# Summing two halves of the squared features on TensorE instead of GpSimd, in the last stage of a fused sequence kernel

## The chip, the cores and the metric

The kernel runs on one core of one Trainium2 chip. The metric is the device time of one execution in microseconds (us); lower is better. The core has five engines that work side by side, each through its own instructions in order: TensorE (PE, with its weight loads listed as PEld), VectorE (DVE), ScalarE (ACT), GpSimd (POOL) and SyncE (SP), which issues DMAs. They wait for each other on semaphores.

## The reference, cut to what matters

Four blocks work on 16 sequences of 256 tokens with 128 channels. The last one, which takes two thirds of the time, is six layers of local attention with l2-normalised queries and keys, and a gated feed-forward layer:

```python
def l2norm(t):
    return t / jnp.maximum(jnp.linalg.norm(t, axis=-1, keepdims=True), 1e-12)

def attn_layer(x, Wqkv, qs, ksc, Wo):
    qkv = x @ Wqkv                      # 16 heads of 64 features for q, k, v
    q, k, v = jnp.split(qkv, 3, -1)
    ...
    q = l2norm(q) * qs
    k = l2norm(k) * ksc
    ...                                 # rotary, scaled by position
    out = local_attention(q, k, v)      # windows of 32, each looks one back
    return out @ Wo

for i in range(DEPTH):                  # DEPTH = 6
    x = attn_layer(shift_tokens(x), ...) + x
    x = ffn_layer(shift_tokens(x), ...) + x
```

The norm of each query and key needs the sum of the squares of its 64 features. That sum is what the change touches.

## The kernel before, in words

The last stage ("phase d") takes the 6 layers times 16 sequences as 96 items n. Every engine runs a loop over turns f, and in a turn works on several items at different steps: the projection of item f and of item f-1, the attention of f-2 and f-3, the feed-forward of f-3 and f-4. The order of the work within a turn is written out by hand, one list of calls for each engine. Nothing is scheduled at run time: an engine goes through its list and stands still at a call whose semaphore isn't there yet.

For one item the projections come in 8 chunks (`CHUNKS`), 4 for keys and 4 for queries. A chunk is a bank of PSUM, 128 rows by 512: 4 heads with 32 features each in the rows, and in the columns two halves of 256 tokens, features 0 to 31 and features 32 to 63 of the same heads. The sum of squares runs through these calls:

- `project` (PE, L1516): 6 matmuls into the chunk's bank.
- `squares` (ACT, L1286): squares the whole bank into one of four buffers `d_sq[i % 4]`, 128 by 2 halves by 256; signals `s_sq`. For the second four chunks it waits until the first four have been summed (`s_sm`).
- `add_halves` (POOL, L1449): adds the second half of the buffer onto the first, 128 by 256; signals `s_sa`.
- `sum_squares(n, m)` (PE, L1527): for the four chunks of `m`, four matmuls with a 128x32 stationary matrix of ones and zeros (`sel`), which add up the 32 rows of each head. Each writes its own 32 columns of the array (`tile_position=(0, g * WIN)`) and its own 32 rows of bank 7. Both values of `m` accumulate there. Signals `s_sm`.
- `norm_rsqrt` (ACT, L1294 to L1296), `norm_weight`, `norm_factor`, `norm_split` (DVE, L1069, L1075, L1082) and `spread_norms` (PE, L1538) turn the sums into factors for the keys, which `scale_keys` (DVE, L1097) applies.

POOL also adds the two products of the rotary step (`rotary_sums`, L1441), scales the scores (`scale_shifted`, L1458), and scales the probabilities (`softmax_scale`, L1464). `rotary_products` (DVE, L1061) waits for `rotary_sums` three chunks back. The rotated queries and keys go to their places by DMAs from SP (L1757 for keys, L1766 for queries), and `scores` (PE, L1549, L1556) waits for them.

In PE's list a turn begins with `turn_tokens` (L1503). `sum_squares(f - 1, 1)` stands before `attention(f - 3, 1)` (L1601), and `sum_squares(f, 0)` between `token_products(f - 2, 5)` and `token_products(f - 2, 6)` (both L1583). `token_products(., 6)` waits for `ffn_scale` of DVE (L1154) as well. Where a new layer begins, ACT and POOL have extra work in their lists: `weights_high`, `tables`, `head_matrices` and `split_low`.

Of the kernel before, what the change touches and what calls it, by code (L numbers as in the profile page):

```python
# [21 lines left out]
ALU = mybir.AluOpType  # L22
# [4 lines left out]
SEQS, T = 16, 256  # L27
# [8 lines left out]
WIN = 32  # L36
# [35 lines left out]
def build(nc, dram, out):  # L72
    ctx = ExitStack()
    with ctx:
        def sb(name, shape, dt=F32):
            return ctx.enter_context(nc.sbuf_tensor(name, shape, dt))
# [5 lines left out]
        bank = [psum[:, i, :] for i in range(8)]  # L82
# [11 lines left out]
        sel = sb("sel", [P, 2, WIN])  # L94
# [708 lines left out]
        def phase_c_tensor(pe):  # L803
# [85 lines left out]
            def sequence_turns(n, s, left):  # L889
# [39 lines left out]
        CHUNKS = 8  # L929
        KS = 3  # L930
        d_xt = [ld(T) for _ in range(3)]
        d_sq = [ld(2, T) for _ in range(4)]
# [19 lines left out]
        base_stage = tab_flat[:, 4 * TPS * DH:4 * TPS * DH + 4 * TPS * P].rearrange("p (k t r f) -> p k t r f", k=4, t=TPS, r=4)  # L952

        (s_sel, s_basep, s_base, s_zk, s_normed, s_zero, s_stats, kept,
         s_xtp, s_xt, s_split, s_proj, s_sq, s_sa, s_xh, s_rp, s_ad, s_sm, s_y, s_r, s_zh, s_z, s_rq, s_R, s_mR, s_dk, s_dq,
         s_s, s_sub, s_rm, s_exp, s_inv, s_prob, s_pt, s_u, s_uev, s_at, s_x2, s_x2p, s_xf, s_mean, s_xsq, s_var,
         d_chain, d_act_chain, s_y2, s_xc, s_xn, s_up, s_gl, s_h, s_ffo, s_x_done, s_m, s_mvo, s_whi, s_wlo, s_tab,
         loaded_qk, loaded_sc, loaded_vo, loaded_w1, loaded_w2) = (
            sem("d_" + s) for s in (
                "sel basep base zk normed zero stats kept "  # L960
                "xtp xt split proj sq sa xh rp ad sm y r zh z rq R mR dk dq "
                "s sub rm exp inv prob pt u uev at x2 x2p xf mean xsq var "
                "chain act_chain y2 xc xn up gl h ffo x_done m mvo whi wlo tab "
                "loaded_qk loaded_sc loaded_vo loaded_w1 loaded_w2").split())
# [6 lines left out]
        def at_least(eng, s, count):  # L971

            if count >= 1:
                eng.wait_ge(s, count)

        def here(n):

            return 0 <= n <= LAST

        def layer_of(n):  # L980
            return n // SEQS
# [40 lines left out]
        def split_low(pool, l, *chunks):  # L1022

            for i in chunks:
                pool.wait_ge(s_whi, CHUNKS * l + i + 1)
                hi, staged = split_high(i)
                lo = wqk_split[:, i, 1, :, :].rearrange("p h (r f) -> p h r f", r=4)
                nc.gpsimd.tensor_tensor(lo, staged, hi.bitcast(F32), ALU.subtract).then_inc(s_wlo, 1)
# [402 lines left out]
        def phase_d_gpsimd(pool):  # L1431
            def rotary_sums(n, *chunks):
                if not here(n):
                    return
                for i in chunks:
                    c = CHUNKS * n + i
                    pool.wait_ge(s_rp, c + 1)
                    if i % 4 == 0:
                        at_least(pool, (s_dk, s_dq)[i // 4], 128 * n)
                    t = d_t[c % KS]  # L1440
                    nc.gpsimd.tensor_tensor(d_rot[i // 4][:, i % 4, :, :], t[:, :, 0, :], t[:, :, 1, :], ALU.add).then_inc(s_ad, 1)  # L1441

            def add_halves(n, *chunks):
                if not here(n):
                    return
                for i in chunks:
                    pool.wait_ge(s_sq, CHUNKS * n + i + 1)
                    sq = d_sq[i % 4]
                    nc.gpsimd.tensor_tensor(sq[:, 0, :], sq[:, 0, :], sq[:, 1, :], ALU.add).then_inc(s_sa, 1)  # L1449

            def scale_shifted(n, h):
                if not here(n):
                    return
                pool.wait_ge(s_sub, 2 * n + h + 1)
                pool.wait_ge(s_rq, n + 1)
                e = d_e[h].rearrange("p (w r) k -> p w r k", w=WPT)
                factor = d_rq[:, WPT * h:WPT * h + WPT, :].rearrange("p w (r m) -> p w r m", m=8)[:, :, :, 4:5]
                nc.gpsimd.tensor_tensor(e, e, factor.to_broadcast([P, WPT, QUADS, 2 * WIN]), ALU.mult).then_inc(s_rm, 1)  # L1458

            def softmax_scale(n, h):  # L1460
                if not here(n):
                    return
                pool.wait_ge(s_inv, 2 * n + h + 1)
                nc.gpsimd.tensor_tensor(d_e[h], d_e[h], d_inv[h].unsqueeze(2).to_broadcast([P, 4 * QUADS, 2 * WIN]), ALU.mult)\  # L1464
                    .then_inc(s_prob, 1)

            nc.gpsimd.memset(d_k, 0.0).then_inc(s_zk, 1)  # L1467
            nc.gpsimd.memset(d_u[:, 0], 0.0).then_inc(s_zk, 1)
            for f in range(TURNS_D):
                fresh = here(f) and f and f % SEQS == 0  # L1470
                next_fresh = here(f + 1) and (f + 1) % SEQS == 0
                rotary_sums(f - 1, 0, 1)
                add_halves(f - 1, 4)
                rotary_sums(f - 1, 2, 3)
                add_halves(f - 1, 5)
                rotary_sums(f - 1, 4)
                add_halves(f - 1, 6, 7)
                rotary_sums(f - 1, 5)
                scale_shifted(f - 2, 0)
                rotary_sums(f - 1, 6, 7)  # L1480
                scale_shifted(f - 2, 1)
                if fresh:
                    split_low(pool, layer_of(f), 4, 5, 6, 7)
                add_halves(f, 0, 1, 2, 3)
                if next_fresh:
                    split_low(pool, layer_of(f + 1), 0, 1, 2, 3)
                softmax_scale(f - 2, 0)
                softmax_scale(f - 2, 1)

        def phase_d_tensor(pe):  # L1490
# [29 lines left out]
            def sum_squares(n, m):  # L1520
                if not here(n):
                    return
                pe.wait_ge(s_sa, CHUNKS * n + 4 * m + 4)
                if m == 0:
                    at_least(pe, s_mR, 2 * n)
                for g in range(4):
                    last = nc.tensor.matmul(bank[7][g * WIN:(g + 1) * WIN, 0:T], sel[:, m, :], d_sq[g][:, 0, :],  # L1527
                                            start=(m == 0), stop=(m == 1), skip_group_check=True,
                                            tile_position=(0, g * WIN))
                last.then_inc(s_sm, 1)  # L1530

            def spread_norms(n, h):
# [142 lines left out]
            for k in range(4):  # L1675
                for t in range(TPS):
                    last = nc.tensor.transpose(bank[k][:, t * P:(t + 1) * P], base_stage[:, k, t, :, :].rearrange("p r f -> p (r f)"),
                                               ident[:, :])
# [5 lines left out]
            for f in range(TURNS_D):  # L1684
# [8 lines left out]
                project(f - 1, 7)  # L1693
                scores(f - 2, 1)
                sum_squares(f - 1, 1)
                attention(f - 3, 1)
                if here(f - 2) and (f - 2) % SEQS == 0:
# [14 lines left out]
                project(f, 4)  # L1712
                token_products(f - 2, 5)
                sum_squares(f, 0)
                token_products(f - 2, 6)
                token_products(f - 2, 7)
# [161 lines left out]
        @block.gpsimd  # L1878
        def _(pool):
            with pool.Fori(0, SA) as step:  # L1880
                phase_a_gpsimd_steps(pool, step)
            end_phase(pool, 1)
            phase_d_constants(pool)
            split_first(pool)
            end_phase(pool, 2)
            end_phase(pool, 3)
            phase_d_gpsimd(pool)
            end_phase(pool, 4)
# [112 lines left out]
```

## Time and profile before

| | |
|---|---|
| median of 3 runs | 4386.15 us (4378.98 to 4389.12) |
| the profiled execution's own time | 4383.15 us |
| its span in the profile | 4381.4 us |
| PE busy | 3982.0 us, 91% |
| DVE busy | 3434.9 us, 78% |
| ACT busy | 2610.2 us, 60% |
| POOL busy | 2353.6 us, 54% |

These shares are over the whole span. The last stage begins at about 1457 us; before it POOL has hardly anything to do. So the stage has to be read by itself. A busy PE is one that has a matmul under way; the ends of matmuls are modelled, so the start of one group of matmuls to the start of the next is a better measure of what a group takes than the sum of its durations. A float32 matmul leaves two records in the trace: four matmuls of `sum_squares` are a row with x8.

### The profile page before, as it was taken

Reading aid. Unit: us, or ns where it says so; the run is one execution under the profiler, and the core shown is the slowest. Engines: PE = TensorE matmul, PEld = TensorE weight load, DVE = VectorE, ACT = ScalarE, POOL = GpSimd, SP = SyncE. Lnnn points to the kernel's source line nnn. Section 1 sums busy time; section 2 is a strip of 40 time slices with the busy share of each in tenths; the row PEclk is TensorE's granted clock in tenths of the full one; section 3 lists DMA queues with packets and bytes.
Section 4 is the critical chain, followed back from the end, with each engine's and each line's share of the span. In section 5 each row is a group of like instructions: output and inputs, shape, how many; then the busy total and the mean of one; then the engine's idle time right before and its main releaser. Section 6 shows DMA issues by size and latency. Waiting matters only on the chain.

```text
span 4381.4 us, 119305 instructions
## 1 busy us (share of the span) xinstructions
PE 3982.0 (91%) x47524; PEld 2662.6 (61%) x47524; DVE 3434.9 (78%) x5294; ACT 2610.2 (60%) x5495; POOL 2353.6 (54%) x2019
## 2 busy tenths in 40 slices
PE   3335998999999599999999999999999999999997
PEld 1112444666666467667676677767666767767765
DVE  6775112666666699998999899989999899989996
ACT  2332333666665466676666666676666666666665
POOL 0001000000000488887888788878888778878884
PEclk7667999999999799999999999999999999999999
DMA  3000000000000233332432332333332343332333
GB/s 100 0 0 0 0 0 0 1 1 0 0 0 1 58 92 69 79 76 65 101 76 64 79 95 67 78 71 91 79 79 64 77 101 69 70 79 68 72 79 78
DMA packets 264306, 238.63 MB, mean 54 GB/s; under 512 B 31494, under 2 KB 259979, under 8 KB 263051
## 3 DMA queue, kind: packets, MB, share of 16 engines
q1 hardware_dynamic: 263818, 231.76, 22.7%
q8 instruction: 352, 5.77, 0.6%
q14 instruction: 136, 1.11, 0.1%
HBM read 26.13 MB, written 4.19 MB: 7 GB/s over the span
## 4 chain that ended last, share of the span: by engine, by line
PE 71%; DVE 4%; ACT 4%; issue 2%; SPq 1%; POOL 1%; DMA 1%; DVEq 0%; ACTq 0%; POOLq 0%
PE bank L1583 15%; PE bank L1516 13%; PE bank L1601 8%; PE bank L1556 7%; PE bank L1643 6%; PE bank L1656 2%; PE bank L1549 2%; PE bank L854 2%; PE bank L819 2%; PE bank L843 2%; PE bank L1527 2%; ACT arena L753 2%; PE bank L832 2%; PE bank L824 2%; PE bank L863 1%
## 5 line engine op out<-in xcount | busy, mean ns | idle before, releaser
L1061 DVE TENSOR_TENSOR arena<-bank,tab 128x1024 f32<-128x1024 f32 x768 | 937.0, 1221 | 193.5 <-ACT arena L1286 135.8
L1441 POOL TENSOR_TENSOR arena<-arena 128x512 f32<-128x512 f32 x768 | 1009.9, 1331 | 42.0 <-DMA arena<-arena 40.6
L1583 PE MATMUL bank<-m_vo,arena 128*32 128x512 f32 x6144 | 756.9, 599 | 17.3 <-DVE arena L1154 11.0
L1286 ACT ACTIVATE arena<-bank 128x512 f32<-128x512 f32 x768 | 457.9, 596 | 526.5 <-PE bank L1516 517.7
L1516 PE MATMUL bank<-x_split,wqk_split 128*128 128x256 f32 x4608 | 720.3, 299 | 25.9 <-DVE arena L1061 11.9
L1516 PEld LDWEIGHTS bank<-x_split,wqk_split 128*128 128x128 f32 x4608 | 605.3, 192 | 175.0 <-issue 85.6
L1449 POOL TENSOR_TENSOR arena<-arena 128x256 f32<-128x256 f32 x768 | 556.3, 735 | 170.1 <-ACT arena L1286 169.8
L1310 ACT ACTIVATE arena<-bank 128x512 f32<-128x512 f32 x768 | 457.0, 596 | 186.4 <-PE bank L1583 183.7
L1467 POOL MEMSET arena<- 128x4608 f32 x1 | 3.9, 3947 | 1039.4 <-DVEq L150 1039.4
L1458 POOL TENSOR_TENSOR arena<-arena 128x1024 f32<-128x1024 f32 x192 | 372.1, 1938 | 262.7 <-DVE arena L1109 262.7
L1464 POOL TENSOR_TENSOR arena<-arena 128x1024 f32<-128x1024 f32 x192 | 373.3, 1945 | 127.3 <-DVE arena L1122 127.0
L1556 PE MATMUL bank<-arena 128*32 128x128 f32 x12288 | 403.7, 273 | 0.4 <-issue 0.4
L1601 PE MATMUL bank<-arena 128*32 128x128 f32 x12288 | 372.1, 273 | 0.0
L1556 PEld LDWEIGHTS bank<-arena 128*32 128x32 f32 x12288 | 345.8, 110 | 37.2 <-issue 0.8
L1601 PEld LDWEIGHTS bank<-arena 128*32 128x32 f32 x12288 | 331.9, 110 | 31.2 <-issue 0.7
L1583 PEld LDWEIGHTS bank<-m_vo,arena 128*32 128x32 f32 x6144 | 158.8, 109 | 260.7 <-ACT arena L1310 140.6
L753 ACT ACTIVATE arena<-bank,arena 128x256 f32<-128x256 f32 x512 | 235.8, 473 | 106.2 <-DVE arena L673 92.1
L1643 PE MATMUL bank<-arena,w 128*128 128x256 f32 (+1 forms) x1152 | 282.2, 381 | 0.9 <-ACT arena L1341 0.8
L398 PE MATMUL bank<-ident,arena 128*128 128x128 f32 x160 | 39.6, 414 | 238.3 <-DVE arena L294 136.7
L1129 DVE STREAM_TRANSPOSE arena<-arena 128x1024 f32<-128x1024 f32 x192 | 235.1, 1224 | 26.6 <-POOL arena L1464 26.6
L1103 DVE TENSOR_REDUCE arena<-bank 128x16 f32<-128x1024 f32 x192 | 234.3, 1220 | 14.3 <-PE bank L1556 6.4
L1097 DVE TENSOR_TENSOR arena<-arena,bank 128x1024 f32<-128x1024 f32 x192 | 232.8, 1212 | 2.7 <-PE bank L1538 2.7
(236 smaller groups left out, 6991.4 us busy)
## 6 DMA issues: line engine op xcount, KB each, us to landing
arena<-arena SPq DMA_DIRECT2D x1536, 128.0 KB, 2.5
wqk_stage<-in_wqk SPq DMA_DIRECT2D x6, 1024.0 KB, 8.3
out_x<-x_all SPq DMA_DIRECT2D x8, 512.0 KB, 4.9
wvt<-in_wvt SPq DMA_DIRECT2D x6, 512.0 KB, 4.3
wo<-in_wo SPq DMA_DIRECT2D x6, 512.0 KB, 5.4
arena<-in_wbh SPq DMA_DIRECT2D x1, 2048.0 KB, 9.4
arena<-out_x SPq DMA_DIRECT2D x4, 512.0 KB, 6.0
w<-in_w SPq DMA_DIRECT2D x6, 341.0 KB, 5.9
```

The source lines that it names most:

```text
L1061: nc.vector.tensor_tensor(d_t[c % KS].rearrange("p k h t -> p k (h t)"), bank[c % 2][:, :].unsqueeze(1).to_broadcast([P, 2, 2 * T]), tab[: ...
L1286: nc.scalar.activation(d_sq[i % 4].rearrange("p h t -> p (h t)"), bank[c % 2][:, :], ACT.Square).then_inc(s_sq, 1)
L1310: nc.scalar.activation(d_u[:, 1 + w, :, :], bank[U_BANK[w]][:, :].rearrange("p (a c) -> p a c", a=QUADS), ACT.Copy).then_inc(s_uev, 1)
L1441: nc.gpsimd.tensor_tensor(d_rot[i // 4][:, i % 4, :, :], t[:, :, 0, :], t[:, :, 1, :], ALU.add).then_inc(s_ad, 1)
L1449: nc.gpsimd.tensor_tensor(sq[:, 0, :], sq[:, 0, :], sq[:, 1, :], ALU.add).then_inc(s_sa, 1)
L1458: nc.gpsimd.tensor_tensor(e, e, factor.to_broadcast([P, WPT, QUADS, 2 * WIN]), ALU.mult).then_inc(s_rm, 1)
L1464: nc.gpsimd.tensor_tensor(d_e[h], d_e[h], d_inv[h].unsqueeze(2).to_broadcast([P, 4 * QUADS, 2 * WIN]), ALU.mult)\
L1516: last = nc.tensor.matmul(bank[c % 2][:, h * T:(h + 1) * T], wqk_split[:, i, wp, h, :], x_split[:, n % 2, xp, :], start=(q == 0), stop=(q ...
L1556: last = nc.tensor.matmul(bank[2 + b][g * WIN:(g + 1) * WIN, (2 * v + a) * P:(2 * v + a + 1) * P], d_q[:, a, g, at:at + WIN], d_k[:, a, g, ...
L1583: last = nc.tensor.matmul(bank[U_BANK[w]][g * WIN:(g + 1) * WIN, :], d_xt[n % 3][:, w * WIN:(w + 1) * WIN], m_vo[:, 4 * g:4 * g + 4, :].re ...
L1601: last = nc.tensor.matmul(bank[6][v * WIN:(v + 1) * WIN, h * C:(h + 1) * C], d_pt[h][:, at, :], d_u[:, WPT * h + v + z, r, :], start=(r == ...
L1643: last = nc.tensor.matmul(bank[UP_BANK[c]][0:m, half * T:(half + 1) * T], w1_of(n)[:, first + c * P:first + c * P + m], d_xn, start=True, ...
```

## The change

`add_halves` is taken out of POOL's list, with its semaphore `s_sa`. `sum_squares` waits for the squares themselves (`s_sq`) and issues eight matmuls in place of four: four over the first halves and four over the second, all in the same accumulation. Nothing else changes.

```diff
-            def add_halves(n, *chunks):
-                if not here(n):
-                    return
-                for i in chunks:
-                    pool.wait_ge(s_sq, CHUNKS * n + i + 1)
-                    sq = d_sq[i % 4]
-                    nc.gpsimd.tensor_tensor(sq[:, 0, :], sq[:, 0, :], sq[:, 1, :], ALU.add).then_inc(s_sa, 1)
...
                 rotary_sums(f - 1, 0, 1)
-                add_halves(f - 1, 4)
                 rotary_sums(f - 1, 2, 3)
-                add_halves(f - 1, 5)
                 rotary_sums(f - 1, 4)
-                add_halves(f - 1, 6, 7)
                 rotary_sums(f - 1, 5)
                 scale_shifted(f - 2, 0)
                 rotary_sums(f - 1, 6, 7)
                 scale_shifted(f - 2, 1)
                 if fresh:
                     split_low(pool, layer_of(f), 4, 5, 6, 7)
-                add_halves(f, 0, 1, 2, 3)
...
-                pe.wait_ge(s_sa, CHUNKS * n + 4 * m + 4)
+                pe.wait_ge(s_sq, CHUNKS * n + 4 * m + 4)
                 if m == 0:
                     at_least(pe, s_mR, 2 * n)
-                for g in range(4):
-                    last = nc.tensor.matmul(bank[7][g * WIN:(g + 1) * WIN, 0:T], sel[:, m, :], d_sq[g][:, 0, :],
-                                            start=(m == 0), stop=(m == 1), skip_group_check=True,
-                                            tile_position=(0, g * WIN))
+                for half in range(2):
+                    for g in range(4):
+                        last = nc.tensor.matmul(bank[7][g * WIN:(g + 1) * WIN, 0:T], sel[:, m, :], d_sq[g][:, half, :],
+                                                start=(m == 0 and half == 0), stop=(m == 1 and half == 1), skip_group_check=True,
+                                                tile_position=(0, g * WIN))
                 last.then_inc(s_sm, 1)
```

PE's list around the second `sum_squares` of a turn (L1527), before; x is the number of matmuls in a row, and `arena` holds all the buffers:

```order
L1656 MATMUL bank<-w,arena 128x128 x6
L1516 MATMUL bank<-x_split,wqk_split 128x256 x6
L1583 MATMUL bank<-m_vo,arena 32x512 x4
L1527 MATMUL bank<-arena,sel 32x256 x4
L1583 MATMUL bank<-m_vo,arena 32x512 x8
L1503 MATMUL bank<-ident,x_all 128x128 x2
```

and the same place of the changed kernel, where the line numbers are 11 or 12 lower (`sum_squares` is L1516 there and `token_products` L1572):

```order
L1645 MATMUL bank<-w,arena 128x128 x6
L1504 MATMUL bank<-x_split,wqk_split 128x256 x6
L1572 MATMUL bank<-m_vo,arena 32x512 x4
L1516 MATMUL bank<-arena,sel 32x256 x8
L1572 MATMUL bank<-m_vo,arena 32x512 x8
L1491 MATMUL bank<-ident,x_all 128x128 x2
```

The four matmuls have become eight at the same place, and no other row of PE has moved.

POOL's list over one turn, before (L1441 is `rotary_sums`, L1449 `add_halves`):

```order
L1464 TENSOR_TENSOR arena<-arena 128x1024 x2
L1441 TENSOR_TENSOR arena<-arena 128x512 x2
L1449 TENSOR_TENSOR arena<-arena 128x256
L1441 TENSOR_TENSOR arena<-arena 128x512 x2
L1449 TENSOR_TENSOR arena<-arena 128x256
L1441 TENSOR_TENSOR arena<-arena 128x512
L1449 TENSOR_TENSOR arena<-arena 128x256 x2
L1441 TENSOR_TENSOR arena<-arena 128x512
L1458 TENSOR_TENSOR arena<-arena 128x1024
L1441 TENSOR_TENSOR arena<-arena 128x512 x2
L1458 TENSOR_TENSOR arena<-arena 128x1024
L1449 TENSOR_TENSOR arena<-arena 128x256 x4
```

and of the changed kernel (L1450 is `scale_shifted` there, L1456 `softmax_scale`):

```order
L1456 TENSOR_TENSOR arena<-arena 128x1024 x2
L1441 TENSOR_TENSOR arena<-arena 128x512 x6
L1450 TENSOR_TENSOR arena<-arena 128x1024
L1441 TENSOR_TENSOR arena<-arena 128x512 x2
L1450 TENSOR_TENSOR arena<-arena 128x1024
```

Eight additions of a turn are gone, and the six first rotary sums stand next to each other.

## Rows read from the trace of the kernel before

**Rows 1.** Busy time by engine: first turns, steady turns, last turns.

```profile
core 0: us, PE busy (x) PEld busy (x) DVE busy (x) ACT busy (x) POOL busy (x), PEclk, DMA share, GB/s
1457.00:1560.00 103.00, 78.06 (x832) 54.61 (x832) 68.61 (x72) 56.31 (x100) 64.67 (x60) 0.80 0.27 61
1560.00:4293.00 2733.00, 2701.36 (x40280) 1902.49 (x40272) 2492.63 (x3037) 1860.80 (x3510) 2208.58 (x1881) 1.00 0.34 78
4293.00:4381.40 88.40, 64.13 (x948) 42.96 (x944) 48.95 (x65) 40.98 (x70) 29.43 (x21) 0.89 0.29 74
```

**Rows 2.** PE in order of time, one turn: start us, us, line.

```profile
2485.54 0.44 PE L1503 MATMUL bank<-ident,x_all 128*128 128x128 f32 x2
...
2512.49 0.61 PE L1527 MATMUL bank<-arena,sel 128*32 128x256 f32 x8
2512.92 1.90 PE L1583 MATMUL bank<-m_vo,arena 128*32 128x512 f32 x16
2514.75 0.44 PE L1503 MATMUL bank<-ident,x_all 128*128 128x128 f32 x2
...
2526.60 0.60 PE L1527 MATMUL bank<-arena,sel 128*32 128x256 f32 x8
2527.03 1.92 PE L1601 MATMUL bank<-arena 128*32 128x128 f32 x64
```

**Rows 3.** PE's longest waits from 1550 to 4250 us: total, times, longest.

```profile
PE bank L1583 <- DVE arena L1154: 9.9, 10, 1.1
PE bank L1623 <- ACT arena L1310: 4.5, 5, 0.9
```

**Rows 4.** Groups by line in the last stage: busy, mean ns, idle before.

```profile
L1449 POOL TENSOR_TENSOR arena<-arena 128x256 f32<-128x256 f32 x764 | 553.4, 735 | 143.9 <-ACT arena L1286 143.6
...
L1527 PE MATMUL bank<-arena,sel 128*32 128x256 f32 x1536 | 118.2, 382 | 1.5 <-POOL arena L1449 1.5
...
L1527 PEld LDWEIGHTS bank<-arena,sel 128*32 128x32 f32 x1536 | 47.0, 110 | 58.4 <-issue 55.0 <-POOL arena L1449 3.3
```

**Rows 5.** The chain that ended last, around 4240 us: start us, us.

```profile
4232.73 0.43 PE bank L1527 x8
...
4246.84 0.43 PE bank L1527 x8
```

**Rows 6.** Weight loads in order of time, at the second group of rows 2.

```profile
2526.49 0.23 PEld L1527 LDWEIGHTS bank<-arena,sel 128*32 128x32 f32 x8
```

**Rows 7.** PE in order of time, two turns where a layer begins.

```profile
1909.05 0.61 PE L1527 MATMUL bank<-arena,sel 128*32 128x256 f32 x8
1910.57 0.64 PE L1583 MATMUL bank<-m_vo,arena 128*32 128x512 f32 x4 [0.91 <-DVE arena L1154]
...
1940.58 0.61 PE L1527 MATMUL bank<-arena,sel 128*32 128x256 f32 x8
1942.26 1.92 PE L1583 MATMUL bank<-m_vo,arena 128*32 128x512 f32 x16 [1.06 <-DVE arena L1154]
```

**Rows 8.** From the sums to the spread norms, steady turn, in order of time.

```profile
2527.28 0.39 ACT L1294 ACTIVATE arena<-bank 128x256 f32<-128x256 f32 x1 [0.51 <-PE bank L1527]
...
2532.53 0.48 DVE L1082 SCALAR_TENSOR_TENSOR z_split<-z_split,odd,arena 128x256 fp32r<-128x256 f32 x1
...
2533.41 0.48 PE L1538 MATMUL bank<-z_split,sel_r 128*128 128x256 f32 x2
```

**Rows 9.** The chain that ended last, in the first turns of the stage.

```profile
1470.20 1.06 PE bank L1527 x8
...
1478.73 0.73 POOL arena L1449
1479.51 1.12 PE bank L1527 x8
...
1505.73 0.73 POOL arena L1449
```

**Rows 10.** The same chain, where the last item is projected.

```profile
4302.00 0.74 POOL arena L1449
...
4303.57 0.74 POOL arena L1449
```

More of the change, by code:

```diff
@@ L954, in build @@
         (s_sel, s_basep, s_base, s_zk, s_normed, s_zero, s_stats, kept,
-         s_xtp, s_xt, s_split, s_proj, s_sq, s_sa, s_xh, s_rp, s_ad, s_sm, s_y, s_r, s_zh, s_z, s_rq, s_R, s_mR, s_dk, s_dq,
+         s_xtp, s_xt, s_split, s_proj, s_sq, s_xh, s_rp, s_ad, s_sm, s_y, s_r, s_zh, s_z, s_rq, s_R, s_mR, s_dk, s_dq,
          s_s, s_sub, s_rm, s_exp, s_inv, s_prob, s_pt, s_u, s_uev, s_at, s_x2, s_x2p, s_xf, s_mean, s_xsq, s_var,
@@ L960, in build @@
                 "sel basep base zk normed zero stats kept "
-                "xtp xt split proj sq sa xh rp ad sm y r zh z rq R mR dk dq "
+                "xtp xt split proj sq xh rp ad sm y r zh z rq R mR dk dq "
                 "s sub rm exp inv prob pt u uev at x2 x2p xf mean xsq var "
```

## The prediction

> **What bounds the kernel now.** I read the busy times by stretch first [rows 1]. From 1560 to 4293 us PE is busy for 2701.36 of 2733 us, 99%, at a granted clock of 1.00, that is 2.4 GHz. DVE stands at 91%, POOL at 81%, ACT at 68%. In the stretches ahead of it and behind it PE is busy for three quarters of the time, at mean granted clocks of 0.80 and 0.89: these are waits for a chain through all engines. Only 31.64 us of the long stretch (2733.00 less 2701.36) have no matmul.
>
> Busy time alone isn't proof, since ends of matmuls are modelled. So I read PE in order of time [rows 2]. One turn takes 29.21 us (from 2485.54 to 2514.75), and its groups start one behind the other with no wait listed. The list of PE's waits agrees: between 1550 and 4250 us the longest two entries are 9.9 us and 4.5 us in total [rows 3], 10 and 5 times, at the beginnings of layers. And the chain that ended last goes through `sum_squares` itself, 0.43 us each time [rows 5]. The reader is to see a PE that sets the pace, with an addition on POOL that nobody on the path waits for: PE's matmuls of `sum_squares` waited for it for 1.5 us and their weight loads for 3.3 us, over the whole stage [rows 4].
>
> **The change part by part.**
>
> *Removed: 768 additions of POOL*, 735 ns each [rows 4], about 564 us of POOL's time and nearly 6 us of a turn. In the steady turns it is worth nothing, since POOL isn't what PE waits for. What it can give there is at most the few microseconds just named.
>
> *Removed: the wait on `s_sa`*, replaced by one on `s_sq`, which comes earlier. It adds no wait. Behind `sum_squares` in PE's list stand `attention` and `token_products`; neither waits more than before.
>
> *Added: four matmuls in each of 192 calls.* The trace has four such matmuls as one group of 8 records. From its start to the start of the next group it takes 0.43 us, at both places of the turn (2512.49 to 2512.92 and 2526.60 to 2527.03) [rows 2], though each record alone lasts 382 ns [rows 4] and there are eight: the four column strips run together. The second four have the same shape, the same strips and no wait ahead of them, so I take 0.43 us for them too. The nearest bounds: 0.38 us, one record, if nothing is lost between them; and 0.48 us, a quarter of the 1.92 us of the 16 records of 512 columns that are the dearest form of this pattern (`token_products` has 1.90 here [rows 2], 1.92 in another turn [rows 7]). Their eight weight loads fall into 0.23 us while other matmuls run [rows 6].
>
> Where a group at the slower clock stood, it took 1.06 us [rows 9]; an added half there is 0.85 us, twice 0.43.
>
> How many of the 192 lie on the path? The steady turns f = 4 to 95 have two each, 184. Of the first four turns, those at 1543 and 1558 us are in the stretch that PE sets by then. That is 186 x 0.43 = **80.0 us**.
>
> *Given back at new layers.* Five times a layer begins, and twice each time `token_products(., 6)` stands waiting for DVE's L1154 directly behind `sum_squares`: the next group comes 1.52 us and 1.68 us after it and not 0.43 [rows 7]. What is late there is ACT, with its extra work, and DVE behind it, and both depend on matmuls that stand before `sum_squares`. The longer sum fills part of that wait: 10 x 0.43 = 4.3 us back. The bound is the whole 11.7 us (5 x (1.09 + 1.25)), if DVE also came earlier for want of POOL's work.
>
> *The norms chain.* ACT's L1294 waits for the sums each turn [rows 8], so the chain to `spread_norms` starts 0.43 us later. So does the work of PE in between, which stands behind the sums too. DVE's L1082 ends at 2533.01, 0.4 us ahead of L1538 at 2533.41, and this distance stays. Nothing.
>
> *First turns.* Two sums lie on the path at the slow clock: +1.7 us. One addition of POOL comes off ahead of the second, -0.7 us [rows 9]. Later four additions of about 0.7 us, the last of them at 1505.73, stand in POOL's chain behind the first DMAs; PE and ACT run close beside it, so I take half of 2.8: -1.4. Together -0.4 us, between -1.8 and +1.7.
>
> *Last turns.* Two additions of 0.74 us are on the path [rows 10]; the added half of the last sum stands beside them. I take -0.7 us, between 0 and -1.5.
>
> Sum: 80.0 - 4.3 - 0.4 - 0.7 = **+74.6 us**. Against the profiled execution's own 4383.15 us (1.75 us of it outside the span) that is 4457.8 us. That execution lies 3.0 us under the median of the runs shown, which themselves spread over 10 us; I say **4458 us**, 1.6% slower.
>
> **The rivals.**
>
> *Weight loads come into the open: about 4540 us.* The four added matmuls need their own weight loads, 110 ns each [rows 4]. If the second four could not be loaded while the first four stream, an added half would cost 0.43 + 4 x 0.11 = 0.87 us, 186 of them 161.8 us, less the 5.4 us given back: 4383.15 + 156.4 = 4539.6. Against it: the eight loads of a group already lie within 0.23 us and the group still takes 0.43 [rows 2, 6]. The Trainium skill's page "TensorE: Matmul & The Clock Gate" (Part 3: Packing small matmuls) says that a load overlaps matmuls in flight only when its row group differs; here all matmuls use all 128 rows, and by that rule this rival would hold. By that rule the trace does not agree: its 8 loads beside 0.43 us are there already. Chance 5%.
>
> *PE's idle time takes part of it: about 4431 us.* If the 31.64 us without a matmul [rows 1] were slack that closes up, 80.0 - 31.6 = 48.4 us would be left, with the ends of the stage as in my sum about 47.3, so 4430.5. Against it: apart from the waits of rows 3 this idle time lies in small gaps of every turn, between groups of different shape, and a longer group doesn't close them. Chance 4%.
>
> *It is faster: about 4350 us.* The turn could be set by the loop through squares, POOL's addition, sums and norms and only look like PE, with the second halves all but free in the array. Then the turn would lose its idle time and nothing would be added: 4383.15 - 31.6 - 1.1 = 4350.5. It decides from an added half below 0.17 us (31.6 / 186). For it speaks only that the ends of matmuls are modelled. Against it: POOL's addition is waited for by PE for under 5 us in the whole stage, and 0.43 us from start to start is not modelled. Chance 2%. As a weaker form, halves at about 0.17 us give no change at all, 2%.
>
> **How the numbers follow.** My case has 87%, the rivals 5, 4, 2 and 2. The predicted time is that of my case. Its own bounds: low, all the waits at new layers vanish (7.4 us more back) and first and last turns give all (2.2 us): 4448; high, each half at 0.48 us (9.3 us more) and nothing given back at the ends (2.8 us): 4470. With the spread of the runs shown, -4 and +3 us, this is 4444 to 4473, which holds the time 8 times in 10 without reaching to the rivals. A measurement of this kernel tells about 0.2% from no change. Faster 2%, same 2%, slower 96%.
>
> **What would show it.** The matmuls of `sum_squares` double from 1536 to 3072 records, and start to start the group goes from 0.43 to 0.86 us. The steady turn goes from 29.21 to 30.07 us. POOL's busy time falls by about 564 us to 1790, and its idle time grows by more than that, with PE still at 99% between turns 4 and 95. DVE and ACT wait longer for PE's L1516 and L1583 (their numbers before). The waits for L1154 fall from 9.9 us to about 5.6. I would be wrong if the turn grew by less than 0.7 or more than 1.0 us, or if the group took 0.86 us and the turn did not follow it.

## The result, and the profile after

The changed kernel takes 4450.67 us (median of 4 runs, 4446.28 to 4454.78) against 4384.65 us before (4 runs, 4378.98 to 4389.12): a ratio of 1.0152, 95% interval 1.0138 to 1.0166. It is 66 us slower. I had said 4458 us, 1.6% slower, in a range of 4444 to 4473.

The profiled execution of the changed kernel took 4454.78 us. Busy times over its whole span, and the busy times by stretch, cut at the same turns as [rows 1] (first turns up to 1565.5 us, steady turns):

```profile
span 4453.0 us, 121609 instructions
...
PE 4065.0 (91%) x49060; PEld 2710.3 (61%) x49060; DVE 3361.7 (75%) x5294; ACT 2612.4 (59%) x5495; POOL 1781.9 (40%) x1251
```

```profile
1464.10:1565.50 101.40, 80.26 (x888) 54.78 (x888) 66.03 (x72) 56.63 (x100) 45.20 (x32) 0.80 0.28 63
1565.50:4365.00 2799.50, 2775.59 (x41742) 1945.86 (x41742) 2423.05 (x3036) 1862.21 (x3508) 1659.00 (x1145) 1.00 0.33 76
```

POOL has lost 571.7 us of work (2353.6 less 1781.9), and next to nobody was waiting for it. In the steady turns PE is busy 99% as in [rows 1], DVE has fallen from 91% to 87%, POOL from 81% to 59%.

PE in order of time over one turn, the lines that answer to [rows 2] (start us, us, line; `sum_squares` is L1516 here, the first matmuls of a turn L1491):

```profile
2691.67 0.44 PE L1491 MATMUL bank<-ident,x_all 128*128 128x128 f32 x2
...
2703.53 1.04 PE L1516 MATMUL bank<-arena,sel 128*32 128x256 f32 x16
2704.40 1.92 PE L1590 MATMUL bank<-arena 128*32 128x128 f32 x64
...
2719.06 1.05 PE L1516 MATMUL bank<-arena,sel 128*32 128x256 f32 x16
2719.93 1.90 PE L1572 MATMUL bank<-m_vo,arena 128*32 128x512 f32 x16
2721.76 0.44 PE L1491 MATMUL bank<-ident,x_all 128*128 128x128 f32 x2
```

A sum takes 0.87 us from start to start at both places (0.43 before), and the turn 30.09 us (29.21 before); over the whole stage most turns are 30.07 or 30.08 us. The distances between the other groups of the turn have kept to 0.02 us.

Two more views answer to [rows 4] and [rows 3]: the group of `sum_squares` with its busy time, mean ns and idle time, and PE's longest waits from 1560 to 4320 us.

```profile
L1516 PE MATMUL bank<-arena,sel 128*32 128x256 f32 x3072 | 202.7, 383 | 0.7 <-ACT arena L1286 0.7
```

```profile
PE bank L1612 <- ACT arena L1310: 4.5, 5, 0.9
PE bank L1572 <- ACT m_vo L1378: 3.4, 5, 0.7
PE bank L1572 <- DVE arena L1154: 3.1, 5, 0.6
```

The records have doubled. The waits for DVE's L1154 have fallen from 9.9 us in 10 to 3.1 us in 5. Where a layer begins, of the two places in [rows 7] the first has lost all of its listed wait, and the second two fifths of it, 1.06 to 0.63 us (PE in order of time; the next group comes 1.13 and 1.68 us after the start of the sum):

```profile
1923.74 1.05 PE L1516 MATMUL bank<-arena,sel 128*32 128x256 f32 x16
1924.87 1.49 PE L1572 MATMUL bank<-m_vo,arena 128*32 128x512 f32 x12
```

```profile
1955.32 1.05 PE L1516 MATMUL bank<-arena,sel 128*32 128x256 f32 x16
1957.00 1.49 PE L1572 MATMUL bank<-m_vo,arena 128*32 128x512 f32 x12 [0.63 <-DVE arena L1154]
```

The two profiles differ in one more thing, which isn't the change. The last stage begins at 1464.10 us after and 1457.04 us before, 7.06 us apart, and the code up to there is the same. PE in order of time at the end of the stage ahead, before:

```profile
1430.91 2.02 PE L863 MATMUL bank<-arena 128*128 128x128 f32 x16 [0.56 <-ACT arena L765]
...
1433.27 2.05 PE L863 MATMUL bank<-arena 128*128 128x128 f32 x16
```

and the same instructions of the changed kernel:

```profile
1433.90 3.75 PE L863 MATMUL bank<-arena 128*128 128x128 f32 x16 [0.57 <-ACT arena L765]
...
1438.30 3.78 PE L863 MATMUL bank<-arena 128*128 128x128 f32 x16
```

The granted clock of that stretch (1430 to 1435 us) was 1.00 before and 0.50 after, 2.4 and 1.2 GHz. PE had stood still for up to 1.9 us at a time ahead of it before, and for up to 2.4 us after. In the seven experiments below the stage begins between 1455.78 and 1458.95 us. So the stage itself, with what is behind it, is longer by 4453.0 - 4381.4 - 7.06 = **64.5 us** in the profiles. The changed kernel's runs lie in two pairs, at 4446 to 4447 and at 4454 to 4455 us, 8 us apart; that a stretch at the lower clock parts them is likely, since the mean granted clock was 0.956 in both of the slower ones and 0.959 and 0.960 in the faster, but only one of the four has a trace.

### The profile page after: what moved, and what is told of

It is laid out like the page before. It is cut to its first block, busy times and chain, and to the rows that moved or that the text cites. A ratio compares the mean times of both kernels' runs of the same rounds, so it can differ in the third digit from the quotient of the medians.

```text
span 4453.0 us, 121609 instructions
## 1 busy us (share of the span) xinstructions
PE 4065.0 (91%) x49060; PEld 2710.3 (61%) x49060; DVE 3361.7 (75%) x5294; ACT 2612.4 (59%) x5495; POOL 1781.9 (40%) x1251
## 3 DMA queue, kind: packets, MB, share of 16 engines
q14 instruction: 129, 1.06, 0.1%
## 4 chain that ended last, share of the span: by engine, by line
PE 74%; ACT 4%; DVE 4%; issue 2%; DMA 0%; SPq 0%; ACTq 0%; DVEq 0%
PE bank L1572 15%; PE bank L1504 14%; PE bank L1590 8%; PE bank L1545 8%; PE bank L1632 6%; PE bank L1516 4%; PE bank L1645 3%; PE bank L1538 2%; PE bank L854 2%; PE bank L819 2%; PE bank L843 2%; ACT arena L753 2%; PE bank L832 2%; PE bank L863 2%; PE bank L824 1%
## 5 line engine op out<-in xcount | busy, mean ns | idle before, releaser
L1441 POOL TENSOR_TENSOR arena<-arena 128x512 f32<-128x512 f32 x768 | 966.0, 1285 | 144.4 <-DVE arena L1061 84.8
L1572 PE MATMUL bank<-m_vo,arena 128*32 128x512 f32 x6144 | 755.2, 598 | 10.1 <-DVE arena L1154 4.3
L1450 POOL TENSOR_TENSOR arena<-arena 128x1024 f32<-128x1024 f32 x192 | 372.5, 1940 | 657.3 <-DVE arena L1109 657.3
L1310 ACT ACTIVATE arena<-bank 128x512 f32<-128x512 f32 x768 | 456.9, 596 | 209.9 <-PE bank L1572 207.2
L1456 POOL TENSOR_TENSOR arena<-arena 128x1024 f32<-128x1024 f32 x192 | 373.7, 1947 | 422.8 <-DVE arena L1122 422.8
L1572 PEld LDWEIGHTS bank<-m_vo,arena 128*32 128x32 f32 x6144 | 159.1, 109 | 252.2 <-ACT arena L1310 105.0
L1632 PE MATMUL bank<-arena,w 128*128 128x256 f32 (+1 forms) x1152 | 280.7, 380 | 1.1 <-ACT arena L1341 0.8
L1109 DVE TENSOR_TENSOR arena<-bank,arena 128x1024 f32<-128x1024 f32 x192 | 233.2, 1215 | 0.0
```

The lines of the kernel that those rows point to most:

```text
L1310: nc.scalar.activation(d_u[:, 1 + w, :, :], bank[U_BANK[w]][:, :].rearrange("p (a c) -> p a c", a=QUADS), ACT.Copy).then_inc(s_uev, 1)
L1572: last = nc.tensor.matmul(bank[U_BANK[w]][g * WIN:(g + 1) * WIN, :], d_xt[n % 3][:, w * WIN:(w + 1) * WIN], m_vo[:, 4 * g:4 * g + 4, :].re ...
L1632: last = nc.tensor.matmul(bank[UP_BANK[c]][0:m, half * T:(half + 1) * T], w1_of(n)[:, first + c * P:first + c * P + m], d_xn, start=True, ...
```

## The experiments

Theory: PE sets the steady turn, each added group of four matmuls costs its start-to-start time, and POOL's additions are worth only what they give at the ends and at new layers. Rival: the turn is set by a loop through POOL's addition. A third question is why the second halves cost 0.43 us and not more. For each run the length of a steady turn is the median of the 91 turns 4 to 94, from the start of the first matmuls of one to the next; turns at new layers are given as so many us above it.

**The matmuls alone** (`sums_both`). The kernel before, with both halves in `sum_squares` and POOL's additions kept:

```diff
                 pe.wait_ge(s_sa, CHUNKS * n + 4 * m + 4)
...
-                for g in range(4):
-                    last = nc.tensor.matmul(..., sel[:, m, :], d_sq[g][:, 0, :], ...
+                for half in range(2):
+                    for g in range(4):
+                        last = nc.tensor.matmul(..., sel[:, m, :], d_sq[g][:, half, :], ...
```

> The kernel before with the eight matmuls of sum_squares, but GpSimd's additions and the wait on s_sa kept (the second halves are counted twice, so the norms are others). My theory, that TensorE sets the turn: a steady turn of 30.07 us as in the changed kernel, 0.86 us from the start of a sum to the next group, and a time within 15 us of the changed kernel's. What GpSimd's relief gives shows as the difference between the two at new layers and in the first turns: if the waits there come from the GpSimd work, turns at new layers are as far above the steady turn as before (1.12, 2.48, 4.73 us above it); if they are merely filled by the longer sum, they are as in the changed kernel (0.30, 2.05, 4.37 us above it). The rival, a turn set by a loop through GpSimd, wants a turn longer than 30.07 us here, by up to the 0.735 us of an addition.

Measured: 4452.59 us, ratio to before 1.0160 (1.0143 to 1.0177). The steady turn is 30.07 us. Turns at new layers are 0.70, 2.07 and 4.37 us above it. All of the slowdown is in the matmuls; no loop through POOL sets the turn. The waits lie between my two cases: the second and third are as in the changed kernel, so the longer sum fills them, the first only in part.

**The removal alone** (`sums_none`). The changed kernel with four matmuls over the first halves:

```diff
                 pe.wait_ge(s_sq, CHUNKS * n + 4 * m + 4)
...
-                for half in range(2):
-                    for g in range(4):
-                        last = nc.tensor.matmul(..., d_sq[g][:, half, :], ...
+                for g in range(4):
+                    last = nc.tensor.matmul(..., d_sq[g][:, 0, :], ...
```

> The changed kernel with four matmuls in sum_squares, over the first halves only (the squares of the second halves are left out of the norms). GpSimd's additions are gone and TensorE has no more to do than before. My theory: steady turn 29.21 us as before, and a gain of 1 to 12 us against the kernel before, from the first turns, the last ones and the waits at new layers. The rival, a turn set by a loop through GpSimd, wants a turn below 29 us and tens of us of gain.

Measured: 4375.55 us against 4382.4, ratio 0.9983 (0.9974 to 0.9993), 7 us. The steady turn is 29.21 us, as before. PE in order of time at a new layer, the place of the first pair of [rows 7] (`sum_squares` is L1515 here):

```profile
1905.13 0.61 PE L1515 MATMUL bank<-arena,sel 128*32 128x256 f32 x8
1906.24 1.92 PE L1571 MATMUL bank<-m_vo,arena 128*32 128x512 f32 x16 [0.49 <-DVE arena L1154]
```

The wait for L1154 is 0.49 us instead of 0.91, with the sum as short as before. Here POOL's absence helps: the turn is 0.70 us above the steady one and not 1.12. At the second place it doesn't (2.48 us, as before); at the third it is 4.37 us in four turns of five, before 4.73.

What POOL's additions do to DVE shows in one instruction, L1049 (`split_low_tokens`, which reads two operands from SBUF). Its durations, min/median/max in ns, of the kernel before and of this run:

```profile
L1049 DVE TENSOR_TENSOR x_split<-arena,x_split x96: 426/1355/1447, 1459.1 to 4277.3; 128x256 fp32r<-128x256 f32 x96
```

```profile
L1049 DVE TENSOR_TENSOR x_split<-arena,x_split x96: 414/417/1214, 1457.9 to 4268.0; 128x256 fp32r<-128x256 f32 x96
```

The median is 1357 ns in `sums_both` and 416 in the changed kernel. With the additions in POOL's list this instruction runs beside POOL's L1458 and L1441 in 94 of 96 turns; without them POOL's list has run ahead, and in 52 of the 96 turns here no POOL instruction stands beside it for more than 0.05 us. These 0.94 us of a turn are about half of DVE's fall from 91% to 87%; the longer turn is the other half. A steady turn gains nothing from them, since DVE isn't what PE waits for there. That they are what shortens the wait for L1154 is likely; it wasn't tried by itself.

**One more group** (`sums_three`):

```diff
-                for half in range(2):
+                for k, half in enumerate((0, 1, 1)):
...
-                                                start=(m == 0 and half == 0), stop=(m == 1 and half == 1), ...
+                                                start=(m == 0 and k == 0), stop=(m == 1 and k == 2), ...
```

> The changed kernel with twelve matmuls in sum_squares, the last four over the second halves once more (they count twice in the norms). If TensorE sets the turn and an added group of four costs its 0.43 us every time: 1.29 us a sum, a steady turn of 30.07 + 0.86 = 30.93 us, and about 75 us above the changed kernel. The waits at new layers behind the second sum of a turn should shrink by another 0.4 us each: from 0.30 and 2.05 us above the steady turn to about 0 and 1.65.

Measured: 4524.95 us in one run. PE in order of time at the end of a steady turn, where the sum takes 1.30 us, and at the second place of a new layer:

```profile
2745.34 1.48 PE L1516 MATMUL bank<-arena,sel 128*32 128x256 f32 x24
2746.64 1.90 PE L1572 MATMUL bank<-m_vo,arena 128*32 128x512 f32 x16
```

```profile
1960.30 1.48 PE L1516 MATMUL bank<-arena,sel 128*32 128x256 f32 x24
1961.98 1.92 PE L1572 MATMUL bank<-m_vo,arena 128*32 128x512 f32 x16 [0.20 <-DVE arena L1154]
```

The steady turn is 30.93 us, as expected. The wait for L1154 goes 1.06, 0.63, 0.20 us with 4, 8 and 12 matmuls in front of it: the sum fills it step by step, and the turn is 2.48, 2.05 and 1.60 us above the steady one. The first place has no wait left.

**The loops exchanged** (`halves_inside`):

```diff
-                for half in range(2):
-                    for g in range(4):
+                for g in range(4):
+                    for half in range(2):
```

> The changed kernel with the two loops of sum_squares exchanged: both halves of one chunk directly behind each other, on the same strip of 32 columns, then the next chunk. Same matmuls, same result. If four matmuls share one stream time because they stand on four strips and matmuls start in order, pairs on one strip follow each other: two streams for the first pair and one more for each later pair, 5 x 0.43 = 2.1 us for a sum and not 0.86, a turn of about 32.6 us and a time about 238 us above the changed kernel's. If the array takes them in any order, nothing changes: 30.07 us.

Measured: 4459.76 us in one run, and my figure of 238 us more was wrong. The steady turn is 30.16 us. PE in order of time:

```profile
2704.64 1.08 PE L1516 MATMUL bank<-arena,sel 128*32 128x256 f32 x16
2705.51 1.75 PE L1590 MATMUL bank<-arena 128*32 128x128 f32 x56
```

Two matmuls on one strip, one behind the other, don't hold up the ones for other strips. That left two readings, and the next run parts them.

**The added matmuls on one strip** (`one_strip`):

```diff
                     for g in range(4):
+                        to = 0 if half else g
-                        last = nc.tensor.matmul(bank[7][g * WIN:(g + 1) * WIN, 0:T], sel[:, m, :], d_sq[g][:, half, :],
+                        last = nc.tensor.matmul(bank[7][to * WIN:(to + 1) * WIN, 0:T], sel[:, m, :], d_sq[g][:, half, :],
...
-                                                tile_position=(0, g * WIN))
+                                                tile_position=(0, to * WIN))
```

> The changed kernel with the four added matmuls of a sum all on the first strip of 32 columns, accumulating into the first 32 rows (the sums of the second halves go to the wrong rows). The run with the loops exchanged took no more time for pairs on one strip, so it isn't settled whether the strips run side by side. If they do, each strip working through its own matmuls, the first strip has five of the eight: 5 x 0.43 = 2.1 us a sum, a steady turn of 30.07 + 2 x 1.28 = 32.6 us and about 4690 us. If a matmul of 32 columns simply costs a quarter of the time wherever it stands, nothing changes: 0.86 us and 30.07 us.

Measured: 4687.71 us in one run, with a steady turn of 32.63 us. PE in order of time, one sum (`sum_squares` is L1517, `attention` L1591):

```profile
2798.33 2.11 PE L1517 MATMUL bank<-arena,sel 128*32 128x256 f32 x15
2800.06 0.42 PE L1591 MATMUL bank<-arena 128*32 128x128 f32 x6
2800.27 0.38 PE L1517 MATMUL bank<-arena,sel 128*32 128x256 f32 x1
2800.49 1.74 PE L1591 MATMUL bank<-arena 128*32 128x128 f32 x56
```

The reader is to see two things. The sum takes 2.16 us from 2798.33 to 2800.49, five times 0.43, for eight matmuls of the same shape: each strip works through its own matmuls, and the fullest one sets the time. And six records of `attention` start before the last record of the sum, on strips that are free. But they start only at 2800.06, 1.73 us (four times 0.43) after the start of the sum, while three of the strips had one matmul each, 0.43 us of work. So a full strip does hold up the others' next call, here for 1.3 us; with no more than two matmuls on each strip (`halves_inside`) it didn't. How many it takes wasn't measured.

**Cheaper sums, without POOL** (`squares_bf16`). The result pointed to PE's time as the only thing worth saving:

```diff
-        sel = sb("sel", [P, 2, WIN])
+        sel = sb("sel", [P, 2, WIN], BF16)
...
-        d_sq = [ld(2, T) for _ in range(4)]
+        d_sq = [ld(T).bitcast(BF16).rearrange("p (h t) -> p h t", h=2) for _ in range(4)]
```

> The changed kernel with the squares written as bfloat16 by ScalarE and summed against a bfloat16 matrix of ones (the squares are rounded to 8 bits; the sums still gather in float32). The four bfloat16 matmuls with 512 columns in scores take 0.22 us from start to start, so eight with 256 columns should take about 0.22 us, against 0.43 before and 0.86 in the changed kernel. My theory, TensorE sets the turn: steady turn 29.21 - 2 x 0.21 = 28.8 us, and a time about 4384 - 186 x 0.21 - 8 = 4337 us, 1.1% below the kernel before. If DVE or ScalarE then sets the turn, it stays above 28.8 us and their waits for TensorE fall.

Measured: 4345.08 us, ratio to before 0.9916 (0.9900 to 0.9933): faster than both kernels, by 37 us and by about 106 us. (The two profiles of this run and of before lie 39.2 us apart: 32.0 us in the turns 4 to 94, 7.6 us in the first turns, where the clock also steps at other points.) PE in order of time at the end of a turn:

```profile
2668.13 0.40 PE L1516 MATMUL bank<-arena,sel 128*32 128x256 bf16 x8
2668.35 1.90 PE L1572 MATMUL bank<-m_vo,arena 128*32 128x512 f32 x16
2670.18 0.44 PE L1491 MATMUL bank<-ident,x_all 128*128 128x128 f32 x2
2670.49 1.96 PE L1632 MATMUL bank<-arena,w 128*128 128x256 f32 x8
2672.39 0.40 PE L1538 MATMUL bank<-mask_bf,ident_bf 128*32 128x512 bf16 x4
```

The sum takes 0.22 us, as expected, but the turn is 28.90 us and not 28.8. Behind the shorter sum the first matmuls of the turn take 0.31 us to the next group (0.28 in the changed kernel), and L1632 behind them 1.90 (1.82). DVE isn't what holds them: its `ffn_residual` (L1170), the call that the turn's first matmuls wait for, ends 0.78 us ahead of them.

```profile
2669.04 0.36 DVE L1170 TENSOR_TENSOR x_all<-x_all,bank 128x256 f32<-128x256 f32 x1
```

L1632 is `ffn_up`, and its first matmuls wait on `s_uev` for ScalarE's L1310 (`read_products` for `token_products(., 6)`, the call behind the sum). ScalarE in order of time from `token_products(., 5)`, the call ahead of the sum, on, with PE's start of that call and the weight loads of L1632:

```profile
2667.25 1.07 PE L1572 MATMUL bank<-m_vo,arena 128*32 128x512 f32 x8
2668.38 0.60 ACT L1310 ACTIVATE arena<-bank 128x512 f32<-128x512 f32 x1 [1.15 <-PE bank L1572]
2668.88 0.50 ACT L1341 ACTIVATE arena<-arena,cols_d 128x256 f32<-128x256 f32 x1
2669.27 0.59 ACT L1286 ACTIVATE arena<-bank 128x512 bf16<-128x512 f32 x1
2669.75 1.16 ACT L1310 ACTIVATE arena<-bank 128x512 f32<-128x512 f32 x2
2670.46 1.59 PEld L1632 LDWEIGHTS bank<-arena,w 128*128 128x128 f32 x8
```

ScalarE has no pause from 2668.38 us to the end of the first of the two L1310, and 0.11 us behind that end (2670.35) the loads begin: 3.21 us from 2667.25 to 2670.46. The same distance is 3.31 us in the kernel before (2511.61 to 2514.92) and 3.75 in the changed one, where PE itself is the later. So at this place only 0.10 us of the shorter sum counts, and 0.21 at the other: 29.21 - 0.10 - 0.21 = 28.90 us. ScalarE is the next limit there, by these rows; no run made ScalarE's part alone shorter.

**Cheaper sums, with POOL's additions** (`gpsimd_bf16`). The kernel before, with POOL writing its sums as bfloat16:

```diff
+        d_sb = [ld(T // 2).bitcast(BF16) for _ in range(4)]
...
-                    nc.gpsimd.tensor_tensor(sq[:, 0, :], sq[:, 0, :], sq[:, 1, :], ALU.add).then_inc(s_sa, 1)
+                    nc.gpsimd.tensor_tensor(d_sb[i % 4], sq[:, 0, :], sq[:, 1, :], ALU.add).then_inc(s_sa, 1)
...
-                    last = nc.tensor.matmul(..., sel[:, m, :], d_sq[g][:, 0, :],
+                    last = nc.tensor.matmul(..., sel[:, m, :], d_sb[g],
```

> The kernel before, with GpSimd's additions kept but written as bfloat16 to four buffers of their own, and four bfloat16 matmuls a sum against a bfloat16 matrix of ones (each sum of two squares is rounded to 8 bits). A sum should take 0.11 us from start to start instead of 0.43, half of the 0.22 of eight bfloat16 matmuls. If TensorE alone sets the turn: 29.21 - 2 x 0.32 = 28.57 us and about 4384 - 60 = 4324 us, below the bfloat16 squares with GpSimd's additions removed (turn 28.90, 4345). If the waits that the shorter sums uncover count more, for DVE's ffn_scale and ScalarE's step behind it, with GpSimd at work too: a turn of 28.8 to 29.1 us and 4340 to 4375 us.

Measured: 4355.52 us, ratio to before 0.9940 (0.9923 to 0.9956), as in my second case. A sum takes 0.11 us, the least of all runs, and the median turn is 28.80 us. ScalarE's chain gives this turn too (L1584 is `token_products` here, L1644 `ffn_up`):

```profile
2672.32 1.06 PE L1584 MATMUL bank<-m_vo,arena 128*32 128x512 f32 x8
...
2675.54 1.59 PEld L1644 LDWEIGHTS bank<-arena,w 128*128 128x128 f32 x8 [0.20 <-issue]
```

From 2672.32 to 2675.54 it is 3.22 us again, though the sum between is half as long, and 29.21 - 0.10 - 0.32 = 28.79. Yet the run takes 10 us more than the one without POOL's additions. PE's longest waits from 1560 to 4250 us:

```profile
PE bank L1584 <- DVE arena L1155: 13.1, 10, 1.4
PE bank L1517 <- DVE arena L1062: 7.9, 20, 0.7
```

With the shortest sum PE waits for DVE at new layers 13.1 us (L1155 is `ffn_scale` here; 10.0 us in `squares_bf16`) and 20 times for the rotary products (7.9 us; 2.4 us in 7 there). The turns 4 to 94 have 56.0 us above the median turn in all, 41.7 us without the additions: that is where the smaller turn goes. In all these turns take 5.2 us more than without the additions (2676.79 and 2671.59 us). A further 7.1 us lie in the first turns (102.90 and 95.83 us), where the clock steps at other points in each trace; how much of that is POOL's isn't shown.

## Why the prediction was right

The mechanism of the steady turn held, and the time came within 8 us. The smaller terms were less good. By its terms:

*The added halves.* 0.43 us each, for the reason given. In the trace the 91 turns from 4 to 95 went from 2703.58 to 2770.36 us (first to last start, 1560.44 to 4264.02 and 1565.53 to 4335.89). Of that, 91 times the growth of a steady turn is 79 us; my term has 78.3 for these 182 halves. `sums_both` and `sums_three` show the same step, twice. The price rests on four strips side by side, which I had only read off two rows; `one_strip` shows it.

*Given back at new layers.* Here is what was mis-sized: 4.3 us in the sum, 12.4 us measured (the stretch grew by 66.8 us and not by 79.2). The part I named is right: two waits behind the sum are filled by 0.4 us each, five times. I missed three:

- The first of these waits also shrinks when POOL's additions are gone, by another 0.42 us: 1.12 us above the steady turn before, 0.70 with either part of the change alone, 0.30 with both. It was in my bound, and I had set it at nothing. Five times, 2.1 us. This is also why the waits for L1154 fell to 3.1 us and not to 5.6.
- The turn with the head matrices has a third wait, 4.73 us above the steady turn before and 4.36 after. Either part of the change alone gives it. Five times, 1.9 us.
- Single stalls outside that pattern, 0.1 to 1.5 us each, about 4 us in the profiled execution of before, aren't there after. They are hardly there in `sums_both` either (0.3 us beside its new layers), and some 2 us are left in `sums_none`. But `halves_inside`, whose turns are longer still, has 1.8 us of them in two turns, and `sums_three` 1.3 us in two. So they differ from trace to trace, and that the change takes them away isn't shown: about 8 of the 12.4 us are the change's, the rest may be chance.

*First turns.* I had +0.5 us with the halves that lie there, and measured -2.0 (103.40 to 101.43 us). `sums_none` gives -2.6 us and `sums_both` -0.2, which points to POOL's additions. But `halves_inside`, with the same matmuls and without the additions, has 102.82 us here and not 101.43: the clock steps up at other points in each trace, this term stays uncertain by 1 or 2 us, and what POOL's additions were worth in it stays open.

*Last turns.* +0.2 us expected with the added halves, -0.3 measured (117.38 to 117.11 us from the last turn's start to the end of the span).

In all +74.6 us expected for the stage and +64.5 measured, of 66 in the medians. The sum was too high by 10 us, above all by what is given back. That my 4457.8 us came so near to the profiled execution's 4454.78 is luck: 7.06 us of that lie ahead of the stage.

*The rivals.* Weight loads in the open would have made an added half 0.87 us, a sum 1.30 us and the turn 30.9 us. I had priced four loads for it; the rows have eight loads for four matmuls, so it should have been 0.43 + 8 x 0.11 = 1.31 us an added half, and further off still. They stayed hidden. By the rule of the Trainium skill's page "TensorE: Matmul & The Clock Gate" (Part 3: Packing small matmuls) that I cited with that rival, the trace doesn't agree after the change either: 16 loads, all with 128 rows, beside 0.87 us of a sum. Weight loads in order of time at the second sum of the turn shown above:

```profile
2718.64 0.13 PEld L1516 LDWEIGHTS bank<-arena,sel 128*32 128x32 f32 x4 [0.30 <-issue]
2719.07 0.56 PEld L1516 LDWEIGHTS bank<-arena,sel 128*32 128x32 f32 x12 [0.30 <-issue]
```

A turn set by a loop through POOL is ruled out by `sums_none`. PE's idle time did take part of the addition, but little of it: it was 31.6 us in the steady turns and is 23.9 us after (2799.50 less 2775.59). What closed up is waits, while the gaps between groups of the steady turn stayed. That rival and my case were the same mechanism at two sizes.

## What to carry to other kernels

When one engine's groups start one behind the other with no wait between them, work moved onto it costs its full start-to-start time in every turn, and the engine relieved gives next to nothing back, however busy it was: 572 us of GpSimd's time bought 7 us here, 79 us of TensorE's cost 66. The way to use TensorE for the addition was to make the matmul cheaper first: with the squares in bfloat16 the same change beats both kernels. Most of that gain is the cheaper matmul's (29 us with GpSimd's additions kept, 37 without). A shorter group pays in full only until another engine's chain is the later one, here ScalarE's, 0.10 us away. And when a term for waits given back is worked out, every turn of an unusual length should be listed, each with its wait, and not only the ones directly behind the edit.

## What the runs showed of the hardware

- Matmuls on the four strips of 32 columns ran side by side, and the number on the fullest strip set the time of a sum: 0.87 us with two each, 2.16 us with five on one. The order of the eight over the strips, with two on each, made 0.08 us of a turn's difference. With five on one strip, the next call's matmuls for the free strips started 0.2 us before the last record of the sum, but 1.3 us after their strips had run out of work.
- A bfloat16 group of four such matmuls took 0.11 us, a quarter of the 0.43 us in float32.
- A VectorE instruction with two SBUF operands (128x256) took 416 ns in the median of the changed kernel and 1355 ns in that of before, where it ran beside two of GpSimd's instructions on SBUF: taking work from GpSimd shortened VectorE's by 0.94 us a turn.
- Two executions of the same instructions came 7 us apart, 0.16%, ahead of the stage, with a granted clock of 0.50 in one over the stretch from 1430 to 1435 us and 1.00 in the other: the same 16 records took 3.75 us and 2.02 us.
